# Latent attention: the output projection turned, one product per block of features and run of tokens

## The reference

```python
x = x + tanh(g_xattn[0]) * latent_attention(layernorm(x), ctx_512, ...)   # this case
x = x + tanh(g_ffn[0]) * ternary_int8_ffn(layernorm(x), ...)
x = x + tanh(g_xattn[1]) * causal_attention(layernorm(x), ctx_512, ...)
x = x + tanh(g_ffn[1]) * moe_ffn(layernorm(x), ...)
```

## Time and profile before

| | us |
|---|---|
| median of 3 runs (1974.61 to 1982.51) | 1975.31 |
| the profiled execution | 1973.56 |
| its span | 1971.5 |
| TensorE busy | 1792.5 (91%) |
| VectorE busy | 1330.2 (67%) |
| ScalarE busy | 915.1 (46%) |
| GpSimd busy | 603.5 (31%) |

### The profile page before, as it was taken

How to read it: one execution, slowest core, us unless ns; L and a number is a source line. 1 busy time by engine, 2 the same in 40 slices (tenths; PEclk the granted TensorE clock), 3 DMA queues, 4 the chain that set the end, 5 groups by cost and what they waited for, 6 DMA issues and landing times. The chain is left out here.

```text
span 1971.5 us, 30319 instructions
## 1 busy us (share of the span) xinstructions
PE 1792.5 (91%) x10858; PEld 1390.5 (71%) x10858; DVE 1330.2 (67%) x2787; ACT 915.1 (46%) x1989; POOL 603.5 (31%) x582
## 2 busy tenths in 40 slices
PE   5899999999999999999996998899978789999996
PEld 4677877778777777777773544566646778888895
DVE  6777677776787778887786896477755633444563
ACT  3544445433543445444443554555435224555563
POOL 5332122331733122331211130232221354333443
PEclk9999999999999999999997999899989899999998
DMA  5022202210221311222016111000013167788773
GB/s 209 17 87 85 67 35 71 87 58 34 73 88 37 130 62 36 99 95 87 29 38 258 35 39 41 21 1 1 1 63 127 50 189 215 241 275 277 234 225 72
DMA packets 51401, 191.77 MB, mean 97 GB/s; under 512 B 7519, under 2 KB 11743, under 8 KB 39991
## 3 DMA queue, kind: packets, MB, share of 16 engines
q1 hardware_dynamic: 41126, 170.14, 24.2%
q0 software_dynamic: 9840, 19.70, 5.2%
q10 hardware_dynamic: 288, 0.00, 0.0%
HBM read 158.29 MB, written 31.51 MB: 96 GB/s over the span
## 5 line engine op out<-in xcount | busy, mean ns | idle before, releaser
L365 POOL TENSOR_TENSOR la_q_roped<-la_q_roped 128x400 f32<-128x400 f32 x128 | 137.5, 1095 | 671.6 <-DVE la_q_roped L827 671.6
L724 ACT ACTIVATE la_probs<-banks,la_minus_max 100x361 f32<-100x361 f32 x256 | 144.5, 564 | 197.3 <-DVE la_minus_max L917 197.3
L827 DVE TENSOR_TENSOR la_q_roped<-banks,la_rope_q 128x400 f32<-128x400 f32 x384 | 196.6, 565 | 23.2 <-PE banks L475 13.3
L529 PEld LDWEIGHTS banks<-identity,la_probs 100*121 100x121 f32 x768 | 113.1, 184 | 71.0 <-DVE la_probs L924 45.6
L924 DVE TENSOR_SCALAR la_probs<-la_probs,la_rsum 100x361 f32<-100x361 f32 x256 | 153.8, 601 | 9.1
L2175 DVE TENSOR_TENSOR ex_weights_low<-ex_raw_weights,ex_weights_high 128x2048 fp32r<-128x2048 f32 x39 | 89.4, 2292 | 95.0 <-ACT ex_weights_high L2066 92.4
L540 PE MATMUL banks<-la_probs_t,la_kv_rows 121*128 121x200 f32 x768 | 151.4, 333 | 0.0
L529 PE MATMUL banks<-identity,la_probs 100*121 100x100 f32 x768 | 126.0, 272 | 21.9 <-DVE la_probs L924 18.4
L917 DVE TENSOR_REDUCE la_minus_max<-banks 100x1 f32<-100x361 f32 x256 | 135.0, 527 | 14.6 <-PE banks L520 7.9
L540 PEld LDWEIGHTS banks<-la_probs_t,la_kv_rows 121*128 121x128 f32 x768 | 131.5, 189 | 1.8
L742 ACT COPY la_probs_t<-banks 121x300 f32<-121x300 f32 x256 | 105.6, 413 | 51.6 <-PE banks L529 51.2
(11 more groups left out here) (371 smaller groups left out, 5044.8 us busy)
## 6 DMA issues: line engine op xcount, KB each, us to landing
ex_raw_weights<-w_exp SPq DMA_DIRECT2D x39, 1024.0 KB
la_weights<-w_pack SPq DMA_DIRECT2D x15, 1856.0 KB, 7.6
residual<-w_exp SPq DMA_DIRECT2D x24, 1024.0 KB, 7.7
la_kv_turned<-w_ffn SPq DMA_DIRECT2D x30, 384.0 KB, 3.4
la_rope_k<-w_ffn SPq DMA_DIRECT2D x30, 384.0 KB, 3.6
qf_sign_weights<-ffn_signs SPq DMA_DIRECT2D x3, 2048.0 KB, 8.9
ffn_signs<-la_ffn_signs SPq DMA_DIRECT2D x30, 192.0 KB, 2.1
out<-ex_block_out POOLq DMA_DIRECT2D x13, 256.0 KB
```

The source lines that it names most:

```text
L365: pool.tensor_tensor(roped[:, h, 0, c, :], roped[:, h, 0, c, :], roped[:, h, 1, 1 - c, :], ALU.add).then_inc(b_add, 1)
L529: mm = pe.transpose(ps[0:LC, T_BANK, c * S:(c + 1) * S], prob[:, j % 4, c * LC:(c + 1) * LC], core.ident[0:S, 0:S])
L724: act.activation(prob[:, s % 4, 0:L], ps[0:S, s % 2, 0:L], ACT.Exp, bias=nmax[:, s % 4:s % 4 + 1], accum_out=sums[:, s % 4:s % 4 + 1]).the ...
L827: dve.tensor_tensor(roped[:, h, v, c, :].rearrange("p (b s) -> p b s", b=GB), ps[:, B_BANKS[k % 2], 0:NT].rearrange("p (b s) -> p b s", b=GB),
```

## The change

`out` is turned: M becomes stationary (128 x 128 slices of it, k = 0 to 3) and ctx moves, some 400 tokens at once: run 0 has 384 and run 1 416 tokens in the first half, 352 and 448 in the second (CUTS). A pass has 2 x 4 products of 6 matmuls, so 48 again. x accumulates as its transpose in `x_all` (`delta`; the first pass of a half copies and does not add). ctx_all takes the place in memory of `roped`. Run 0's products stand in slots 15 to 18 (13 to 16 in pass 7), run 1's in the front of the next pass, after `widen(n,0,0)` and `widen(n,0,1)`; in passes 7 and 15 they stand after the loop. The next pass's first two units come in quarters of 3 matmuls, one each in slots 6 to 11, and the last two quarters after the loop; pass 7 keeps slots 17 and 21. The loop has 20 slots, 23 in pass 7. The FFN weights' sign chunks move from slots 16 to 20 to slots 8, 9, 13 and 14.

x_mid is gone. The untouched x is loaded again as packed tiles (`x_rows`), each tile of the sum is transposed back (`turn_tile`, 4 transposes) and added (`finish_tile`): tiles 0 to 5 in slot 9 to 11 of passes 8 to 13, tiles 6 to 12 after pass 15's loop. Tiles 0 to 2 are loaded in SyncE's turn n = 9 after a wait for the last `turn_x`, since they overwrite rows of x.

```diff
-        SCALE_AT, SIGN_AT = (ITEMS, ITEMS + 2), (ITEMS + 2, ITEMS + 4)
-        MIX, OUT = 5, 8
-        SLOTS = OUT + ITEMS - 1
-        AHEAD = (SLOTS - 6, SLOTS - 2)
+        SCALE_AT, SIGN_AT = (8, 13), (9, 14)
+        MIX = 5
+        AHEAD = (17, 21)
+        FIRST_AT = range(6, 6 + KC + KC // 2)
+        TILE_AT = 9
...
+        def slots(n):
+            return range(AHEAD[1] + 2 if ends_half(n) else MIX + 2 * HB - 1)
...
                 for n in range(2, RUNS + 1):      # SyncE
                     refill_sums(n - 1)
                     refill_signs(n - 2, slice(3, None))
+                    if n == PAIRS + 1:
+                        sp.wait_ge(x_t, B)
+                        for t in range(3):
+                            load_tile(t)
...
-                    if n == PAIRS + 2:
-                        sp.wait_ge(o_add, PAIRS * HB)
-                        core.store_rows(sp, x_mid, 0)
-                    if n == PAIRS + 3:
-                        core.load_packed(sp, x_mid, 0)
                     sp.wait_ge(k_psum, (n - 1) * UNITS)
                     if ends_half(n - 2):
                         sp.dma_start(raw_all, ctx_in[1]).then_inc(kv_loaded, 16)
...
+                def out(n, run, k):
...
+                    kc = slice(k * 128, (k + 1) * 128)
                     for h in range(2):
-                        for j, (a, c) in enumerate(((ch, mh), (ch, ml), (cl, mh))):
-                            mm = pe.matmul(ps[0:S, O_BANK, :], a[:, b % 2, h, :], c[:, h, :],
+                        for j, (a, c) in enumerate(((mh, ch), (ml, ch), (mh, cl))):
+                            mm = pe.matmul(ps[:, out_bank(n, run, k), 0:count], a[:, h, kc], c[:, h, :],
...
+                def turn_tile(t):
...
+                    for k in range(KC):
+                        mm = pe.transpose(ps[0:n, tile_bank(t), k * 128:(k + 1) * 128],
+                                          core.x_all[:, t, k * 128:k * 128 + n], core.ident[:])
...
                     widen(n, 0, 0)
+                    if early(n) and n:
+                        out(n - 1, 1, 0)
+                        out(n - 1, 1, 1)
                     widen(n, 0, 1)
+                    if early(n) and n:
+                        out(n - 1, 1, 2)
+                        out(n - 1, 1, 3)
...
+                        if s == TILE_AT and tile_of(n) is not None:
+                            turn_tile(tile_of(n))
+                        if s in outs_at(n):
+                            out(n, 0, outs_at(n).index(s))
+                        if s in FIRST_AT and early(n + 1):
+                            first_units(n + 1, FIRST_AT.index(s) // KC, [FIRST_AT.index(s) % KC])
...
+                    if ends_half(n):
+                        for k in range(KC):
+                            out(n, 1, k)
+                    elif early(n + 1):
+                        first_units(n + 1, 1, range(KC // 2, KC))
+                    else:
+                        turn_tile(TILES0)
+                        turn_tile(TILES0 + 1)
+                        for k in range(KC):
+                            out(n, 1, k)
+                        for t in range(TILES0 + 2, PT):
+                            turn_tile(t)
...
                 sp.dma_start(wq[:, GATE, :], w_quant[GATE]).then_inc(loaded[GATE], 16)
-                core.load_packed(sp, x_mid, 3)
                 sp.dma_start(wq[:, UP, :], w_quant[UP]).then_inc(loaded[UP], 16)
-                core.load_packed(sp, x_mid, 4)
```

More of the change, by code:

```diff
@@ L64, in __init__ @@
         self.wscale, self.winv = self.sbuf("ffn_w_scale", [128, 3]), self.sbuf("ffn_w_inverse", [128, 3])
[L65 to L68, removed]
+        self.packed = (range(0, HT // 128), range(HT // 128, PT))
         self.tile_out = [nc.alloc_semaphore(f"x_tile_stored{t}") for t in range(PT)]
@@ L221, in latent_attention @@
         o_psum, o_add = sem("out_psum"), sem("out_added")
+        f_in, f_last = [sem(f"x_tile_in{i}") for i in range(3)], sem("x_last_tiles_in")
+        f_psum, f_add = sem("x_tile_turned"), sem("x_tile_added")
         q_in = [sem(f"ffn_weights_in{i}") for i in range(2)]
@@ L258, in ends_half, with early, unit_bank, outs_at @@
             return n == PAIRS - 1
+        def slots(n):
+            return range(AHEAD[1] + 2 if ends_half(n) else MIX + 2 * HB - 1)
+        def early(n):
+            return n < RUNS and not starts_half(n)
+        def unit_bank(n, u):
+            return A_BANKS[u] if u < 2 and early(n) else u % 2
+        def outs_at(n):
+            lo = 13 if ends_half(n) else 15
+            return range(lo, lo + KC)
+        def out_bank(n, run, k):
+            if run:
+                return LAST_BANKS[k]
+            return (A_BANKS if ends_half(n) else B_BANKS)[k % 2]
@@ new lines, in tokens_of, with ctx_of, pieces @@
+        def tokens_of(n, run):
+            cut = CUTS[n // PAIRS]
+            return (cut, HT) if run else (0, cut)
+        def ctx_of(n, run, low):
+            lo, hi = tokens_of(n, run)
+            each = 2 * (hi - lo)
+            return ctx_all[:, run, low * each:(low + 1) * each].rearrange("p (h s) -> p h s", h=2)
+        def pieces(n, b):
+            for run in range(2):
+                lo, hi = (max(a, c) for a, c in zip(tokens_of(n, run), (b * S, 0)))
+                hi = min(hi, (b + 1) * S)
+                if lo < hi:
+                    yield run, lo - tokens_of(n, run)[0], slice(lo - b * S, hi - b * S)
@@ L563, in pair, with first_units @@
+                def first_units(n, u, blocks=range(KC)):
+                    if 0 in blocks:
+                        pe.wait_ge(w_split, n * 2 + 1)
+                        if not early(n):
+                            pe.wait_ge(s_exp, n * ITEMS + u - 1)
+                        elif u == 0:
+                            pe.wait_ge(m_low, n * 2)
+                        else:
+                            pe.wait_ge(c_done, n * (UNITS // 2))
+                    project(n, u, blocks)
                 def pair(n):
@@ L597, in pair @@
                     wout(n, 1)
-                    for s in range(SLOTS):
+                    for s in slots(n):
                         if s < ITEMS:
```

226 lines of the change are left out of this document (158 added, 68 removed).

## The result

The changed kernel takes 1982.62 us (median of 20 runs, 1979.68 to 1985.64), the kernel before 1977.94 in the same sessions (20 runs, 1973.06 to 1982.63): ratio 1.0022, interval 1.0014 to 1.0031. It is slower by 4.7 us, where 3 us less were forecast. The time lies inside the range of 1963 to 1984, but the change has the other sign.

The account below looks back on a forecast made before the run. TensorE's matmul stream was taken to bound the passes. Passes -27.5, change of halves +25.4 and the end -1.0 gave -3.1 us on the profiled 1973.56, so 1970.5, stated as a median of 1972; range 1963 to 1984, wider 1948 to 1992.

Parts of the forecast that it names:

- Passes: -27.5 us: Fourteen passes, all but 7 and 15: 33.6 us saved on matmuls, less added waits and work, plus front slack, net -27.5 us.
- 48 x 0.05 = 2.4 us a pass: Projection of each pass: 48 matmuls of 400 columns on average take 0.18 us instead of 0.23 for 512.
- In slots 6 to 11 [...] nothing: Slots 6 to 11: each holds a quarter, TensorE has 3.7 us a batch, so no loss to VectorE; 0 us.
- slots 12 to 14 [...] close, but below: nothing: Slots 12 to 14, no quarter or projection: TensorE 2.6 us a batch, VectorE 2.5, so no loss; 0 us.
- The quarters, "nothing": Next pass's first units: quarters instead of whole units change no count, bank and weights are free; 0 us.
- The residual's wait, +0.35: End of the loop: `widen(n+1,0,0)` waits for run 0's last addition, +0.35 us a pass, 4.9 in all.
- the front's slack, -0.5 in six passes: Front: four projections there let half of TensorE's 1.1 us wait for VectorE's rope go in six passes, 3.0 us gained.
- the third rival: Slots 8 to 14: VectorE's ring takes over above 3.2 us a batch, costing 2.4 us a pass; 1999 or 1990 us; 17%.
- The change of halves, +25.4: Pass 7 to 8: context load waits behind the last `turn_x`; narrowing 27.4 us later, -4.5 for earlier `turn_x`, +2.5 for clock.
- The end, -1.0: Pass 15 and next stage: +3.9 added, -1.9 for SyncE's last loads, -3.0 for VectorE's tile wait, together -1.0 us.
- the first: Rival at the change of halves: the context isn't late for TensorE, so no stall; kernel 1942 us; 15%.
- The second: Rival: stall stands, but passes give all of 33.6 + 7 us, last `turn_x` 6.9 earlier, no clock loss; 1957 us; 20%.

Follow-up runs that it names:

- e8: e1 with the six tiles' transposes, addition and bn_stats in passes 8 to 13 cut to a quarter, part of the computation left out; 1955.74 us, ratio 0.9881.
- e1: Changed kernel with SyncE's wait for the last turn_x and the three tile loads put behind the second half's context load; 1957.61 us, ratio 0.9898.
- e9: e5 with the sign chunks of passes 9 to 14 in slots 16 to 19 instead of 8, 9, 13 and 14; 1943.14 us, ratio 0.9817.
- e5: e1 with the six quarters in slots 6, 8, 10, 12, 13 and 14 instead of 6 to 11; 1950.71 us, ratio 0.985.
- e6: e1 without quarters: next pass's first unit whole in slot 10, half the second in slot 12; 1965.54 us, ratio 0.9938.
- e14: Changed kernel, late context load kept, with quarters in slots 6, 8, 10, 12, 13, 14 and sign chunks in 16 to 19; 1972.38 us, ratio 0.9962.
- e2: Kernel before with only SyncE's wait for the last turn_x added ahead of the second half's context load; 2007.09 us, ratio 1.014.
- e13: e9 with the tile turned, added and measured in slots 17 to 19 instead of 9 to 11; 1944.76 us, ratio 0.9827.
- e4: e1 with the sign chunks of passes 9 to 14 in slots 16 to 19 instead of 8, 9, 13 and 14; 1957.32 us, ratio 0.9889.

## Why the forecast was wrong

**The step that failed is the term "Passes: -27.5 us"**: it measured -18.6, and 3.6 of these are a gain that I had not counted. What is left is 15 us. Of the 27.5, 14.4 were for passes 0 to 6, which gave 8.8, and 13.1 for passes 8 to 14, which gave 9.8, or 6.2 without those 3.6. (First scores of passes 2 to 7 came 1.6 us closer on average, 59.4 against 61.1, not 2.0.) The parts:

- *48 x 0.05 = 2.4 us a pass.* The spacing itself was right (0.231 to 0.183 us at 400 columns on average), and the 128-column loads did not show. But in sum `out` went from 11.20 to 9.27 us a pass, 1.93. The spacing holds inside a stream; run 0's four outs in slots 15 to 18 each stand behind a mix or transposes, and their first matmul takes 0.25 to 0.32 us to the next start. 14 x 0.47 = 6.6 us too much.
- *"In slots 6 to 11 [...] nothing", "slots 12 to 14 [...] close, but below: nothing".* This is the other part, and I had the rival for it. A batch of slots 12 and 13 was to take 2.6 us. It takes 1.12 + 1.81 = 2.93 in the first half and 1.77 + 2.17 = 3.94 in passes 9 to 13 (scores to scores). In the first half VectorE is busy 2.46 us of this batch, as I had it (2.5), and the batch is still 0.3 us longer than TensorE's own work: there the busy share did not tell what the chain of row maximum, exponential, copy and transposes takes. In the second half my 2.5 us were too few as well. The tile, the chunks and the low part of the quarters' unit all lie in slots 9 to 14; VectorE is busy 3.35 of the 3.94 us, and 7.75 us in slots 10 to 14 of pass 11, as long as TensorE (7.81); a maximum queued behind 1.25 us of them came 1 us late. And I let the tile's addition and statistics "lie beside", and the chunks cost 0.3; they were worth 0.8 us (tile, e8 against e1) and 0.9 us (chunks, e9 against e5) in a pass of the second half.
- *The quarters, "nothing".* e6 says that cutting them was right in the first half; e5 that their place was wrong. In passes 2 to 6 a quarter makes an odd slot, which has a mix, 0.55 us longer (1.81 to 2.36), and an even slot only 0.23 (1.12 to 1.35). That the even slot otherwise stands waiting for the softmax chain is the likely reason; the view of waits lists none there.
- *The residual's wait, +0.35, and the front's slack, -0.5 in six passes*: measured 0.3, and 0.7 in passes 11 and 12. Right in kind, and near in size.
- *Pass 13*: before did six bn_stats in one go in the next front, 3.6 us. I read the line in the diff and gave it no price; it was in the trace.
- *Pass 9*, also at nothing: it gained 1.8 us, its neighbours 10 to 12 0.4 each. Before, six loads of packed x stand on SyncE's queue from 668.54 on, and in that front VectorE waits for the store of a sign chunk that is issued behind them (674.81), and comes late to its rope:

```profile
681.42 0.56 DVE L860 TENSOR_SCALAR la_ffn_signs<-la_kv_turned 128x768 bf16<-128x768 f32 x1 [2.68 <-DMA ffn_signs<-la_ffn_signs]
```

Pass 10 is 1.7 us shorter and has no such wait. With x_mid gone the loads are gone; no run separates this, so that they are the cause is likely and not shown.

So the third rival was half right: its mechanism, at the place it named, in passes 9 to 13 and not in all. By my terms a pass there was to gain 1.85 us (2.4 - 0.35 - 0.3 - 0.4 + 0.5), and passes 10 to 12 gained 0.41; its price of 2.4 us a pass was too high, and a batch of over 3.2 us is there only (3.94 against 2.93). (By its own terms that price is 2.8 in a pass with chunks, 3 x 0.6 + 1, and 1.8 in one without.) That e14, two lines of placement away, stands at a ratio of 0.9962, where the forecast's was 0.9984, says that the sum failed here: its passes give 31.8, less the 3.6 of the statistics 28.2, with 27.5 forecast. That these are so near is in part luck, since the 28.2 hold pass 9's gain and the `out` that I over-priced.

**The change of halves, +25.4, measured +28.2.** The mechanism is shown from both sides (e1, e2). From the start of the last `turn_x` the context is asked for at +1.9 us (1.8 forecast), has landed at +10.3 (9.0: I gave the tiles ahead of it 0.6, and it is 1.8, near the upper bound of 1.9), the rope ends and `partners` begin at +36.2 (35.8), the narrowing starts at +40.3 (39.9). The clock cost 1.8 us on the narrowing, where I took 2.5 in all. What was off is the last `turn_x`: it comes 1.4 us earlier than before, counted from pass 7's first scores, not 4.5. TensorE waits for ScalarE's copies in pass 7 up to there, as the earlier trace rows had hinted, 3.5 us now and 1.6 before, and another 1.5 us for the addition of `out`.

The Trainium skill's page "TensorE: Matmul & The Clock Gate", section "HAM oscillation — how this bites in real kernels", has a stall cost a restart at half rate. The trace agrees: clock 0.50 in the standstill, 4.69 us against 2.91 for the narrowing behind it. Its section "Back-to-back issue gap" gives an isolated matmul N/2.4 + 2.5 ns, 169 and 216 ns for 400 and 512 columns, and a sustained 131 ns for 512; the trace has 183 and 231 in a stream. For 512 columns nothing comes near 131; the bf16 matmuls of the next stage have 216.

**The end, -1.0.** Up to the next stage's first transpose +2.3 (+2.0 forecast); behind it -2.8 (-3.0), which is inside what that part varies by with the same code, so this half is neither shown nor refuted.

The other rivals: the context was late for TensorE by 28 us, so the first was wrong; it stood 30 us under the forecast, and e1, which has the context in time, is 25 us under the changed kernel. The second fell with the passes, and with the last `turn_x`, 1.4 us earlier and not 6.9.

What stays open: the 1.2 us a pass that TensorE waits for VectorE's normed probabilities in the first slots are in pass 11 of before, after, e5, e9 and e13 alike; nothing was tried on them. e8's median gave 2 us where its trace gives 5. And the first half's 8.8 instead of 14.4 us is accounted for by trace distances and e5, not by a run for each part.

## What to carry over

A wait put ahead of a load in an in-order queue is priced by following that load to its last user, on every engine; here that gave the way from the last `turn_x` to the narrowing to half a microsecond (39.9 and 40.3), and what it missed was when the last `turn_x` itself comes. A saved matmul is saved only where the chain beside it is shorter still: check it slot by slot, first with all the work that the change puts on each engine there, then with what stands ahead of each link in its engine's order; a busy share of a longer stretch shows neither. Where two engines have a hole at the same place, closing one can show little until the other is closed (0.25 us for the chunks in e4, 0.9 in e9), so a small result there doesn't clear the suspect.

## What I had not expected of the hardware

- Behind the mix, whose operands are plain fp32, the first matmul of a quarter takes 0.32 us to the next start instead of 0.18 (50 cases in the trace of after, mean 0.325); behind scores it takes 0.18. Three quarters a pass stand so, 0.4 us.
- From 352 to 448 columns the spacing follows the columns, 0.161 to 0.204 us, 0.46 ns a column, with no floor to be seen; the weights' load of 128 columns (0.19 us in the trace, beside the matmul) did not set it even at 352.
